# A two-layer graph network: rows of the later tiles grouped by residue modulo 8, smaller last batches, and 18 gathers of the second layer issued in the first

## What is computed

```python
h = relu(layernorm(x))
# layer 1: attention over neighbours, 4 heads of 32
Wh = (h @ W).reshape(N, 4, 32)
e = leaky_relu(s_src[:, None, :] + s_dst[None, :, :])   # s: Wh with a
p = softmax(where(adj > 0, e, -9e15), axis=1)
x = x + elu(sum_j p[i, j] * Wh[j])
# layer 2: maximum over neighbours
h = relu(layernorm(x))
x = x + where(has_neighbour, max_{j: adj[i,j] != 0} h[j], 0)
```

## Time and profile before

| what | value |
|---|---|
| median of 3 runs | 540.37 us (538.02 to 543.01) |
| span of the profiled execution, first to last instruction | 491.0 us |
| stage one, up to stage two's first gather | 297.73 us |
| gathers of stage two, first to last start | 297.73 to 479.15 us |
| busy share of the span: PE, DVE, ACT, POOL | 62%, 64%, 29%, 67% |
| mean granted clock of PE | 0.788 |

### The profile page before, as it was taken

The page is one execution under the profiler, slowest core; times in us unless marked ns, Lnnn a source line. Parts: engine busy times, 40 slices in busy tenths (PEclk is TensorE's granted clock), DMA queues, the critical chain, the costliest instruction groups (busy, mean ns, idle before and its releaser), DMA issues. The chain is left out here.

```text
span 491.0 us, 6636 instructions
## 1 busy us (share of the span) xinstructions
PE 303.5 (62%) x2017; PEld 225.1 (46%) x2017; DVE 314.0 (64%) x1219; ACT 141.5 (29%) x330; POOL 328.1 (67%) x360
## 2 busy tenths in 40 slices
PE   0966567679789687689464521464565655466664
PEld 0833334266346353355354520354564544365653
DVE  6998876859869596779846382455444545454553
ACT  1653422131544538173733160010110101010111
POOL 6972673704777777767777225777777777777770
PEclk9989579689789699788775785588857788875688
DMA  7998699996999999993575011222222222222221
GB/s 263 420 368 348 237 319 380 404 366 237 369 342 371 404 400 404 403 401 124 183 245 165 12 66 53 53 55 53 58 56 63 66 65 64 73 62 75 69 72 45
DMA packets 28731, 100.86 MB, mean 205 GB/s; under 512 B 6869, under 2 KB 13397, under 8 KB 20501
## 3 DMA queue, kind: packets, MB, share of 16 engines
q1 hardware_dynamic: 16245, 76.33, 39.7%
q0 software_dynamic: 9344, 19.75, 15.6%
q10 hardware_dynamic: 3104, 4.33, 2.4%
HBM read 93.92 MB, written 6.46 MB: 204 GB/s over the span
## 5 line engine op out<-in xcount | busy, mean ns | idle before, releaser
L741 POOL DMA_INDIRECT G<-wh_table,idx x146 | 149.1, 1022 | 81.2 <-issue 43.3
L1641 POOL DMA_INDIRECT G<-h_table,idx x146 | 138.2, 946 | 49.1 <-issue 44.2
L1735 DVE TENSOR_TENSOR_SCAN S<-adjf,S,psf 128x512 f32<-128x512 bf16 (+2 forms) x38 | 45.9, 1209 | 85.8 <-PE psf L1666 76.0
L927 PE MATMUL psf<-adjf,packw 128*128 128x512 f16 x256 | 77.4, 446 | 17.5 <-DMA adjf<-in_adj_dram 12.9
L1666 PE MATMUL psf<-identf,G 128*128 128x128 f32 x146 | 31.8, 352 | 81.9 <-DMA G<-h_table,idx 81.9
L1651 ACT COPY Sb<-psf 128x512 f32<-128x512 f32 (+2 forms) x39 | 21.8, 558 | 168.4 <-PE psf L1674 168.4
L1666 PEld LDWEIGHTS psf<-identf,G 128*128 128x128 f32 x146 | 20.0, 173 | 90.4 <-DMA G<-h_table,idx 90.4
L1686 PE MATMUL psf<-Sb,OL 128*128 128x128 f32 x292 | 55.3, 351 | 0.3 <-DVE rows_out L1721 0.2
L1082 PE MATMUL psf<-G,OQ 128*128 128x132 f32 x292 | 48.6, 321 | 7.0 <-issue 5.0
L1686 PEld LDWEIGHTS psf<-Sb,OL 128*128 128x128 f32 x292 | 52.5, 268 | 0.7 <-issue 0.4
L927 PEld LDWEIGHTS psf<-adjf,packw 128*128 128x128 f16 x256 | 24.8, 107 | 55.6 <-issue 17.9
(11 more groups left out here) (188 smaller groups left out, 481.0 us busy)
## 6 DMA issues: line engine op xcount, KB each, us to landing
adjf<-in_adj_dram SPq DMA_DIRECT2D x64, 1024.0 KB, 11.5
adjf<-keep_table SPq DMA_DIRECT2D x4, 960.0 KB, 7.3
G<-wh_table,idx POOLq DMA_INDIRECT x146
G<-h_table,idx POOLq DMA_INDIRECT x146, 2.6
out_dram<-rows_out SPq DMA_DIRECT2D x32, 64.0 KB, 1.7
wh_table<-OQ ACTq DMA_DIRECT2D x7, 272.0 KB, 8.4
h_table<-h1b ACTq DMA_DIRECT2D x3, 384.0 KB, 2.3
xsf<-in_x_dram SPq DMA_DIRECT2D x2, 512.0 KB, 10.3
```

The costliest lines, as they stand in the source:

```text
L741: pool.indirect_dma_start(G[:, plan.at[k] + b, :], None, wh_table, bass.IndirectOffsetOnAxis(ap=idx[:, n:n + 1], axis=0)).then_inc(gathere ...
L927: nc.tensor.matmul(o, packw[:, k, :], bits, start=(k == 0), stop=False)
L1641: pool.indirect_dma_start(G1[:, g % NG, q, :], None, h1_table, bass.IndirectOffsetOnAxis(ap=idx[:, n0 + q:n0 + q + 1], axis=0)).then_inc(f ...
L1735: V.tensor_tensor_scan(S[:, g % 3, 0:w * P], flags[:, n0 * P:(n0 + w) * P], ps[:, g % 3, 0:w * P], start, ALU.mult, ALU.max).then_inc(scan ...
```

## The change

**Rows of the far tiles.** In groups of 88 rows, the first 64 rows of each group go to tiles 16 to 31, the last 24 to tiles 10 to 15. In tiles 16 to 31 each tile holds rows of one residue modulo 8: tiles 16 to 19 and 20 to 23 the residues 0 to 3, 24 and 25 (and 26 and 27) the residues 4 and 5, 28 and 29 (and 30 and 31) the residues 6 and 7. A strip of tile 0 has neighbours of one residue alone. So strips 0 to 3 need no row of tiles 24 to 31, and strips 4 and 5 none of tiles 28 to 31. The price in transfers is that a pass over tiles 16 to 31 now takes more and shorter pieces (x: ten loads, not six; `wh_table`: eleven stores, not nine; `h1_table`: two stores for each of the last two batches).

**Batches.** The cuts are [1, 2, 4, 7, 10, 16, 20, 24, 28, 32]: eleven batches, the last four with four tiles (12 blocks) each.

**Early gathers.** POOL issues the first 18 gathers of stage two (blocks 0 to 17, strips 0 to 5) in stage one, into free room behind the flags in the `adj` buffers: 4, then the powers of batch 9, 8 more, a wait for the store of batch 9's rows, 2, the powers of batch 10, 4. The powers of batch 8 now stand inside the gathers of batch 10. As an index may also point at an unused row, four DMAs from x to `h1_table` on SP's queue, behind the last load of `adj`, fill the rows of tiles 24 to 31 first. Stage two has 128 gathers left, and POOL's waits for PE there start only at group 11.

**Order of the end.** ACT's `h1_out` of batch 8 stands ahead of its copies of batch 9's sums, `h1_out` of batch 9 ahead of the copies of batch 10's. DVE's `finish` is no longer cut in two, and `finish_rest` of batch 9 runs interleaved with `weigh` of batch 10, not behind it. PE's `aggregate` is no longer cut.

```diff
+FAR = 10 * P
+STRIPS = 8
+RESIDUES = [(16, 0, 4), (24, 4, 2), (28, 6, 2)]
 def tile_rows(table, t0, t1):
...
+    far = table[FAR:, :].rearrange("(u r) d -> u r d", r=88)
+    rest = far[:, 64:88, :].rearrange("u (v g) d -> u v g d", v=4)
+    piece(10, 16, lambda i, j: rest[:, :, i:j, :])
+    for first, c, width in RESIDUES:
+        for half in range(2):
+            ranks = far[:, 0:64, :].rearrange("u (v h c) d -> u v h c d", v=4, h=2)[:, :, half, c:c + width, :]
+            piece(first + half * width, first + (half + 1) * width, lambda i, j, ranks=ranks: ranks[:, :, i:j, :])
...
-    cuts = [1, 2, 4, 7, 10, 16, 22, 28, tiles]
+    cuts = [1, 2, 4, 7, 10, 16, 20, 24, 28, tiles]
...
+    EARLY = [plan.unit_block0[4], plan.unit_block0[6]]
...
-        TAKE = [1, 4, 4, 3, 3, 4, 4, 4]
+        TAKE = [1, 4, 4, 3, 3, 4, 4, 3, 3]
...
+            for (_, to), (_, rows) in zip(tile_rows(h1_table, LATE, T), tile_rows(x, LATE, T)):
+                sp.dma_start(to, rows).then_inc(filled, 16)
...
+                few = plan.size[k] <= 12
+                for b in range(plan.size[k]):
...
+                    if b == 8 and k == 1 or b == 9 and k == 2 or b == (5 if few else 7) and 2 < k < NBT - 1:
+                        pool.wait_ge(off_done, k + 2)
+                    if b == 5 and k == NBT - 1:
+                        pool.wait_ge(lines_done, k - 2)
+                    if b == (9 if few else 12) and 2 < k < NBT - 1:
+                        pool.wait_ge(sel_done, k + 2)
+                    if b == 8 and k == NBT - 1:
+                        roots(NBT - 3)
...
+            pool.wait_ge(packed, T)
+            pool.wait_ge(filled, NFILL)
+            pool.wait_ge(h1_stored, h1_count(NBT - 3))
+            early_lines(0, 4)
+            roots(NBT - 2)
+            early_lines(4, EARLY[0])
+            pool.wait_ge(h1_late[0], 16 * len(h1_pieces(NBT - 2)))
+            early_lines(EARLY[0], EARLY[1] - 4)
+            roots(NBT - 1)
+            early_lines(EARLY[1] - 4, EARLY[1])
...
+                if k == NBT:
+                    h1_out(k - 3)
                 sums_out(k - 2)
...
+            elus(NBT - 2)
             exponentials(NBT - 1)
             diagonals(NBT - 1)
-            sums_out(NBT - 1, slice(0, 2))
-            elus(NBT - 2)
-            sums_out(NBT - 1, slice(2, None))
-            h1_out(NBT - 3)
+            h1_out(NBT - 2)
+            sums_out(NBT - 1)
             elus(NBT - 1)
-            h1_out(NBT - 2)
             h1_out(NBT - 1)
...
-                    together(*when(k - 2 < NBT, maxima, k - 2))
-                    if k == NBT + 1:
-                        together(finish(k - 3, 0, 3))
+                    together(*when(k - 2 < NBT, maxima, k - 2), finish(k - 3))
                     together(*when(k - 2 < NBT, less_max, k - 2))
-                    together(*when(k - 2 < NBT, weigh, k - 2))
-                    together(finish(k - 3, 3 if k == NBT + 1 else 0))
-                    together(finish_rest(k - 3))
+                    together(finish_rest(k - 3), *when(k - 2 < NBT, weigh, k - 2))
...
-                if g >= NEAR:
-                    pool.wait_ge(tr_done, g - NEAR + 1)
...
+                if g >= EG + NG:
+                    pool.wait_ge(tr_done, g - NG + 1)
```

More of the change, by code:

```diff
@@ L608, in edge_attention, with h1_pieces @@
         NCONST = 1 + BITS + 8 + 1
-        TAKE = [1, 4, 4, 3, 3, 4, 4, 4]
+        def h1_pieces(f):
+            return tile_rows(h1_table, plan.tiles(f)[0], plan.tiles(f)[-1] + 1) if plan.tiles(f) else []
+        LATE = plan.tiles(NBT - 2)[0]
+        NFILL = 16 * len(tile_rows(x, LATE, T))
+        h1_count = lambda f: 16 * sum(len(h1_pieces(j)) for j in range(1, f + 1))
+        TAKE = [1, 4, 4, 3, 3, 4, 4, 3, 3]
         TAKE += [T - 1 - sum(TAKE)]
@@ new lines, in early_lines @@
+            def early_lines(lo, hi):
+                for n in range(lo, hi):
+                    pool.indirect_dma_start(early[:, n, :], None, h1_table,
+                                            bass.IndirectOffsetOnAxis(ap=idx[:, n:n + 1], axis=0)).then_inc(early_in[n // Q], 16)
+            pool.wait_ge(packed, T)
[4 more added lines that the diff above has]
+            early_lines(4, EARLY[0])
@@ L871, in h1_out @@
                         act.wait_ge(h1_ready, tl[-1] + 1)
[L872 to L873 removed]
+                    stored = h1_stored if f <= NBT - 3 else h1_late[f - (NBT - 2)]
+                    for ts, rows in h1_pieces(f):
+                        act.dma_start(rows, rows_h[:, ts.start - tl[0]:ts.stop - tl[0], :]).then_inc(stored, 16)
             sum_words_to(words_done(-1, POINTS - 1))
```

127 lines of the change are left out of this document (62 added, 65 removed).

## The result

The changed kernel takes 543.17 us, median of 20 runs, where the kernel before takes 540.35 beside it. The ratio is 1.0091, with a 95% interval from 1.0067 to 1.0115: slower by 0.9%, some 4.9 us. The forecast was 528.0, faster by 12.4.

What follows compares the result with a forecast made beforehand. POOL's gathers and their issue were taken to bound the kernel: stage two starts 10.1 us later but loses 22.5, so -12.4 us, a span of 478.6 and 528.0 us against 540.4. The range was 521 to 536.

Steps and rivals of the forecast that it cites:

- The base: Whole kernel: the -12.4 us, from a profile with span 491.0, was set against the median of 540.4, giving 528.0.
- L: Start of POOL's last gather of stage one: 270.74 us before, forecast 273.8.
- Step 1: Stage two: 18 gathers fewer at POOL's pitch of 1.251 us, -22.5 us; the head start gives nothing more.
- Steps 2 to 4: Stage one up to its last gather: +3.0, -1.7, +1.3 and +0.5 us, moving its start from 270.7 to 273.8.
- Step 3: DVE's loop feeding batches of 12 blocks: turn 21.6 to 19.7 us, then 16.9; POOL stalls 1.3 ahead of batch 9.
- Step 2: Stage one on POOL: two more powers ahead of the last gather, +3.0 us; offsets wait of 1.68 gone, -1.7.
- step 4: Start of stage one: four more loads of x delay its last quarter, +0.5 us, between 0 and 1.9; `h1_table` fills cost nothing.
- the rival in which the loop binds: DVE's turn stays near 21.6 us, stalling POOL up to 12 us: 538.7 us; chance 0.12 for losing over 7 us.
- Step 5: From stage one's last gather to stage two's first: 27.0 us becomes 34; stage two starts at 307.8, 10.1 later.
- The sum: Whole kernel: stage two starts 10.1 us later and loses 22.5, together -12.4 us, span 478.6, time 528.0.
- The rival of the stream: New row order slows the `adj` stream for tiles 10 to 31; 9% uses up the gain, 15% gives 548 us; chance 0.05.
- DVE beside the early gathers: DVE's closing chain of stage one: not slowed by gathers beside it; if slowed 8%, the sum is 0.9 us dearer.

Runs made afterwards that it cites:

- half_lines_b: Kernel before with every second gather of stage two left out from the seventh group on, 540 occasion: 454.45 us, ratio 0.8448.
- a_again: The changed kernel unchanged, timed again beside the kernel before on a 492 occasion: 486.98 us, ratio 0.9895.
- after_gate3_b: Changed kernel with stage two's gate at three groups, as before the change, instead of six, on a 492 occasion: 486.92 us, ratio 0.9887.
- gate3_all: Changed kernel with the gate of three groups from stage two's first group not gathered early, on a 492 occasion: 489.68 us, ratio 0.9929.
- b_again: The kernel before, unchanged, timed and profiled once more on a 540 occasion: 539.92 us, ratio 0.9986.
- fours_only: Kernel before with only the batches of four tiles at the end (eleven batches), on a 540 occasion: 550.78 us, ratio 1.0133.
- near_six_b: Kernel before with stage two's gathers allowed six groups ahead of the transposes instead of three, 540 occasion: 545.75 us, ratio 1.011.

## Why the prediction was wrong

**The base.** "Its span is 49.4 us below the median of the runs, which hold what lies ahead of the first and behind the last instruction; that part is taken as unchanged." This step failed, and with it the last line of the sum, which set -12.4 against 540.4. At most 2.0 us lie outside the span; the rest is inside: 21.7 us up to L and 28.0 in stage two, less 2.6 between them. Late results are seen in both parts; how much of the 47 us they make is not shown, and by half_lines_b the long ones are not all. The gap of 49.4 us was read as a constant that has nothing to do with the kernel, and it was the sign that the profile was of an execution in which another thing bounds. On the occasion of the result three terms came out otherwise: L +15.5 in place of +3.1, the piece from L to stage two +12.1 in place of +7, stage two -18.3 in place of -22.5.

**Step 1, stage two, -22.5.** Right where the rows were from: 193.3 us became 170.4 (482.6 - 312.18), -22.9. On the 540 occasion 221.3 became 202.95 (547.4 - 344.45), -18.3. There "the head start gives nothing more" and "it doesn't depend on PE or DVE" don't hold: the wider gate, which the prediction never priced, costs 0.7% in the changed kernel and 1.1% in the kernel before.

**Steps 2 to 4, L +3.1.** On a 492 occasion L moved from 270.74 to 276.63 in a_again, +5.9. But a_again's profiled run is the fastest of its six. Six profiles of 492 occasions have the changed stage one up to L, and in them L is 275.50 to 283.73, 279.1 in the mean; three have the old one (268.83, 270.74 and 271.46), 270.3 in the mean. So L moved by some 8.8 us, nearly three times the forecast, and in two of the six it is beyond the 280 at which the prediction said that the forecast falls. Step 3 was right in the stall and not in the turn: in a_again DVE's indices of batch 9 come 21.0 us after those of batch 8 (19.7 forecast, 21.6 before), those of batch 10 another 17.3, with waits of 1.62 and 0.49 ahead of the batches, where 1.3 and none stood in the sum. (For the second turn 16.9 was written; the step's own terms, 19.7 - 1.5 - 0.7, give 17.5.)

```profile
221.91 0.17 DVE L1431 SCALAR_TENSOR_TENSOR idx<-jq 128x12 int32<-128x12 int32 x1
...
242.90 0.17 DVE L1431 SCALAR_TENSOR_TENSOR idx<-jq 128x12 int32<-128x12 int32 x1
...
260.16 0.17 DVE L1431 SCALAR_TENSOR_TENSOR idx<-jq 128x12 int32<-128x12 int32 x1
```

Step 2 was not right: the wait of 1.68 went, and one of 1.87 to 3.01 for the same offsets came in batch 8. And the new loads of x were undersized: the first gather comes at 46.85 in place of 45.05, 1.8 and not 0.5, the upper end of what step 4 allowed. These make 3.1 + 2.0 + 1.3 = 6.4 in a_again. In the two profiles with the latest L (after_gate3_b, 282.49, and gate3_all, 283.73) a second such wait of 3.04 and 3.93 stands in an earlier batch; why it comes there and not in the others was not settled. On the 540 occasion L moved by 15.5 us (292.47 to 307.99). A third of it is in one row, the 7.41 in batch 8, where b_again's waits of this kind are 2.29 at most; the turn of DVE from batch 8's indices to batch 9's takes 25.6 us there:

```profile
247.50 0.17 DVE L1431 SCALAR_TENSOR_TENSOR idx<-jq 128x12 int32<-128x12 int32 x1
...
273.12 0.17 DVE L1431 SCALAR_TENSOR_TENSOR idx<-jq 128x12 int32<-128x12 int32 x1
```

That resembles the rival in which the loop binds, by another cause: POOL waits for PE's offsets more than for DVE's indices. That its price of up to 12 us is near the 12.4 by which L overshot is luck.

**Step 5, from L to stage two, 27.0 to 34.** 35.55 on the 492 occasion (276.63 to 312.18). The power stood at L + 9.8, not 11.2, the last early gather started at L + 29.2, not L + 31, and yet stage two began 1.5 us later, since some 5 us stand between POOL's own last operation and stage two. The step took the 4.0 us behind the last store (293.72 to 297.73) for the boundary and left 2.0 behind POOL's last gather, where 5.39 were measured. On the 540 occasion the piece grew from 24.4 to 36.5, by 12.1.

**The sum.** On a 492 occasion -8.4 in the two profiled runs and -5.2 to -6.4 by ratio and median, against -12.4: the sign and the mechanism held, the size was half. With the mean L the terms meet the ratio: +8.8 to L, +8.6 from L to stage two (27.0 to 35.6), -22.9 in it, together -5.5. On a 540 occasion the profiled runs give +15.5 + 12.1 - 18.3 = +9.3, of which the ratio confirms 4.9; the rest is within what one profiled run differs from the median (this one took 549.01, its median 543.17).

**The rival of the stream.** PE's packing on the 540 occasion stands 24.7 us idle in all, 17.1 of them for ACT (the group of L991 above), so the stream of `adj` isn't what it waits for, and 9% more on it is out. Still the new rows by themselves cost 1.2% (0.6 to 1.8) there. Where that time goes was not settled; the first gather is 1.8 us later (47.44 against 45.61), but on this kind of occasion it is as late in fours_only (47.05), which has the old rows.

**DVE beside the early gathers.** The trace of a_again has the operation of elu (L1562, four tiles) once with POOL idle and once beside its gathers:

```profile
283.07 0.68 DVE L1562 SCALAR_TENSOR_TENSOR xsf<-ex,xsf 128x512 f32<-128x512 f32 x1
...
297.22 0.69 DVE L1562 SCALAR_TENSOR_TENSOR xsf<-ex,xsf 128x512 f32<-128x512 f32 x1
```

0.68 and 0.69: in this pair the gathers don't slow it, as the sum had it. The Trainium skill, GPSIMD Engine Reference, section 1 (Specifications), expects contention for a DVE instruction with two SBUF inputs; with gathers as POOL's work this trace doesn't show it.

## What to carry to other kernels

A profile whose span doesn't match the median of the runs is a profile of another execution; ask what would bound the kernel if the missing time lay inside it, before anything is summed. Taking work out of the bounding engine's queue gains its pitch only in places where that queue has a hole: work put behind the last wait ahead of a stage's boundary delays the boundary by as much as it saves. And a gate that looks idle in one profile may be what keeps an engine from running ahead at a price: an edit that widens it belongs in the sum.

## What the runs showed that was not expected

The kernel before takes 492 or 540 us, each held for a whole occasion, with no run in between (488 to 497 and 535 to 546), on one chip both. On 540 occasions results of PE come to their readers long after the record has the matmul ended (12.1 us for the sums read at 349.24 in b_again, 25.8 for the transposes read at 366.29 in near_six_b), and the longest stretch in which PE, DVE and ACT all stand still is 8.2 us in b_again, 11.9 in the changed kernel and 13.7 in near_six_b; the granted clock in stage two of b_again is 0.68 of full speed, where the earlier trace rows has 0.74. What delays them is open, and so is whether the result or the matmul itself is late. It isn't the number of PE's instructions, which is the same; it isn't that POOL stands still, for it goes on issuing through such a stretch. The long stretches all but go away with half of the gathers (one over 2.5 us in place of 11, clock 0.82), yet two thirds of stage two's extra time stay; and single ones get longer when gathers may run further ahead (gate of six, ratio 1.011). All that is compatible with gathers and late results being linked, in whichever direction; no run tells that link's nature, and none tells what makes stage one 19 us longer.
